# A routed expert layer: index table, gather and adding scatter in place of stored token rows

## The reference

```python
x = x + xattn(layernorm(x), ctx_768, ...)      # 16 heads over 257 context rows of 384
x = x + attn(layernorm(x), W_qkv, W_o)         # 16 heads of 32, within 32 tokens
x = x + ffn(layernorm(x), gate_w, gate_b, w1, b1, w2, b2, ln_g, ln_b)

def ffn(x, ...):                               # 8 experts, 2 per token
    logits = (x @ gate_w + gate_b) / 0.9
    topk_vals, topk_idx = top_k(logits, 2)
    gate_probs = softmax(where(chosen, logits, -inf))
    h = gelu(einsum('bsd,edf->bsef', x, w1) + b1)          # d 512, f 2048
    expert_out = einsum('bsef,efd->bsed', h, w2) + b2
    out = einsum('bse,bsed->bsd', gate_probs, expert_out)
    return (out - mean) / sqrt(var + 1e-5) * ln_g + ln_b
```

## Time and profile before

| | before |
|---|---|
| median of 3 runs | 1409.48 us (1407.01 to 1409.59) |
| profiled execution, own time | 1407.61 us |
| its span, first to last instruction | 1406.0 us |
| granted TensorE clock, mean | 0.980 |
| TensorE busy (PE) | 1312.6 us, 93% |
| VectorE / ScalarE / GpSimd busy | 1021.6 / 887.6 / 160.4 us |
| moved by DMA | 241.15 MB, 172 GB/s |

### The profile page before, as it was taken

One profiled execution on the slowest core, in us unless ns is written; L12 is line 12 of the kernel. 1 busy time (PEld: TensorE's weight loads), 2 busy tenths in 40 slices (PEclk: granted clock), 3 DMA queues, 4 the chain that ended last, 5 costly groups with the idle time before them and its releaser, 6 DMA issues.

```text
span 1406.0 us, 26769 instructions
## 1 busy us (share of the span) xinstructions
PE 1312.6 (93%) x8412; PEld 856.8 (61%) x8413; DVE 1021.6 (73%) x2163; ACT 887.6 (63%) x1427; POOL 160.4 (11%) x200
## 2 busy tenths in 40 slices
PE   5889999999999999999999789999999999999977
PEld 5658668687686686876866544555554545454532
DVE  5765777876868778768676558777777777778765
ACT  3567776676767776767677145666666666666630
POOL 1002002021020020211200200000000000000014
PEclk9998999999999999999999899999999999999997
DMA  9797245264272451732716980761617074300014
GB/s 366 284 357 259 86 164 203 64 251 145 94 254 82 172 194 64 265 131 96 252 61 226 367 311 17 298 251 62 265 48 278 35 288 176 140 22 22 15 46 149
DMA packets 70482, 241.15 MB, mean 172 GB/s; under 512 B 5422, under 2 KB 5532, under 8 KB 64292
## 3 DMA queue, kind: packets, MB, share of 16 engines
q1 hardware_dynamic: 57232, 156.77, 31.2%
q0 software_dynamic: 13184, 83.89, 15.6%
q10 hardware_dynamic: 28, 0.01, 0.0%
HBM read 177.73 MB, written 62.91 MB: 171 GB/s over the span
## 4 chain that ended last, share of the span: by engine, by line
PE 78%; DVE 8%; issue 5%; ACT 5%; DMA 2%; POOL 2%; ACTq 0%; DVEq 0%; SPq 0%
PE bank L1648 9%; PE bank L1606 8%; PE bank L743 6%; PE bank L745 6%; PE bank L744 6%; PE bank L723 6%; PE bank L724 6%; PE bank L725 5%; PE bank L1569 4%; PE bank L1674 4%; PE bank L1590 3%; PE bank L733 3%; PE bank L1615 2%; PE bank L1630 2%; PE bank L1696 2%
## 5 line engine op out<-in xcount | busy, mean ns | idle before, releaser
L1606 PE MATMUL bank<-moe_w 128*128 128x257 f32 x768 | 188.8, 383 | 6.4 <-DVE moe_w L1025 6.4
L1606 PEld LDWEIGHTS bank<-moe_w 128*128 128x128 f32 x768 | 137.5, 191 | 25.2 <-DVE moe_w L1025 5.8
L723 PE MATMUL bank<-moe_w,arena 128*128 x368 | 139.9, 380 | 0.0
L725 PE MATMUL bank<-moe_w,arena 128*128 x368 | 139.9, 380 | 0.0
L724 PE MATMUL bank<-moe_w,arena 128*128 x368 | 139.9, 380 | 0.0
L1648 PE MATMUL bank<-moe_w 128*128 128x512 f16 x384 | 114.5, 379 | 9.9 <-ACT moe_w L1082 7.0
L464 ACT ACTIVATE wosT<-moe_w,now_v_act 128x1024 f16 x92 | 100.7, 1141 | 27.5 <-PE bank L745 27.5
L554 DVE SCALAR_TENSOR_TENSOR arena<-bank,now_b,arena 128x512 f32<-128x512 f32 x92 | 69.0, 751 | 62.3 <-PE bank L725 55.7
L1068 ACT ACTIVATE moe_w<-bank,cols,ugain 128x512 f32<-128x512 f32 x96 | 74.6, 777 | 61.7 <-PE bank L1649 60.7
L1278 DVE TENSOR_TENSOR moe_w<-bank,moe_w 128x512 f16<-128x512 f32 (+1 forms) x96 | 65.4, 688 | 47.9 <-ACT moe_w L1082 45.6
L457 ACT ACTIVATE arena<-bank,now_h 128x512 f16<-128x512 f32 x92 | 63.6, 691 | 50.4 <-PE bank L733 34.8
(11 more groups left out here) (283 smaller groups left out, 3011.0 us busy)
## 6 DMA issues: line engine op xcount, KB each, us to landing
moe_w<-in_L_ffn_w_dram SPq DMA_DIRECT2D x46, 1024.0 KB, 6.3
moe_w<-w_halves POOLq DMA_DIRECT2D x8, 4096.0 KB, 13.0
moe_w<-in_L_ffn_w_dram POOLq DMA_DIRECT2D x8, 4096.0 KB, 24.5
w_halves<-moe_w SPq DMA_DIRECT2D x48, 512.0 KB, 4.7
xs_rows<-blocks SPq DMA_DIRECT2D x8, 2048.0 KB, 14.6
arena<-in_ctx_dram SPq DMA_DIRECT2D x32, 384.0 KB
arena<-in_L_ffn_w_dram SPq DMA_DIRECT2D x10, 1024.0 KB, 5.0
blocks<-in_L_ffn_w_dram SPq DMA_DIRECT2D x8, 1024.0 KB, 4.8
```

The source lines that it names most:

```text
L723: nc.tensor.matmul(bank[fb % 2][:, :], xT_low[:, k, :], high, start=(k == 0), stop=False)
L725: last = nc.tensor.matmul(bank[fb % 2][:, :], xT_high[:, k, :], low, start=False, stop=(k == KD - 1))
L1606: last = nc.tensor.matmul(bank[h][:, 0:KEYS], qkT[:, c, b, h * P:(h + 1) * P], cnT[:, b % 2, c, :], start=(c == 0), stop=(c == KC - 1))
```

## The change

- Groups: `y2` is stored once, in token order, to `xn_rows` (GpSimd). What is scattered by slot is an entry of 8 bytes: the token's index and its gate, into `slot_table`. The gates are computed per group (`gates`, `gate_exp`).
- Zeroing: instead of `xs_rows`, the accumulator `acc_rows` (1152 rows), the 128 spare rows of `xn_rows`, and the table is preset with indices of spare rows.
- Jobs: GpSimd loads 128 entries of the table per job (23 DMAs, the last 22 between the gathers of jobs 0 and 1), gathers the token rows by them, and adds the result rows into `acc_rows` by an indirect DMA with addition. VectorE adds the expert's bias in `y_copy` and multiplies by the gate in a further instruction (`y_gate`).
- Expert weights are loaded from SyncE's queue.
- End: SyncE loads the eight tiles of `acc_rows`; gathers, diagonal matrices and mixing matmuls are gone.

```diff
@@ moe_loads (SyncE) @@
+            sp.wait_ge(m_full, M_FILLS * GROUPS)
+            sp.wait_ge(sum2_done, KD * GROUPS)
+            for k in range(KD):
+                sp.wait_ge(halves_out[k], 32 * GROUPS)
+            expert_load(sp, 0)
             sp.wait_ge(b_full, B_FILLS * GROUPS)
+            b2_load(sp, 0)
...
+            sp.wait_ge(xs_in, 16)
+            sp.wait_ge(experts_in, 64)
+            expert_load(sp, 1)
+            b2_load(sp, 1)
+            for e in range(2, EXPERTS):
+                sp.wait_ge(experts_in, 64 * e)
+                ended = sp.value_load(end_i[0:1, e - 1:e], min_val=1, max_val=1 + FB * JOBS)
+                sp.wait_ge(mm2_done, ended)
+                expert_load(sp, e)
+                sp.wait_ge(mm2_done, ended + 1)
+                b2_load(sp, e)
+            sp.wait_ge(ys_stored, 16 * JOBS)
+            for t in range(GROUPS):
+                sp.dma_start(got[:, t, :], acc_dram[t * P:(t + 1) * P, :]).then_inc(gathered[t], 16)
@@ moe_pool (GpSimd) @@
+            def idx_load(j, done):
+                row = pool.value_load(job_rows[0:1, j:j + 1], min_val=0, max_val=ROWS // P - 1)
+                pool.dma_start(job_idx[:, j, :], table[bass.ds(row * P, P), :]).then_inc(done, 16)
+            def x_gather(j):
+                nc.gpsimd.indirect_dma_start(
+                    out=xs, out_offset=None, in_=xn_dram[:, :],
+                    in_offset=bass.IndirectOffsetOnAxis(ap=job_idx[:, j, 0:1].bitcast(U32), axis=0)).then_inc(xs_in, 16)
+            def y_add(j):
+                nc.gpsimd.indirect_dma_start(
+                    out=acc_dram[:, :], out_offset=bass.IndirectOffsetOnAxis(ap=job_idx[:, j, 0:1].bitcast(U32), axis=0),
+                    in_=ys, in_offset=None, compute_op=ALU.add).then_inc(ys_stored, 16)
             pool.wait_ge(jobs_ready, 1)
+            pool.wait_ge(scattered, 16 * GROUPS * TOPK)
+            pool.wait_ge(y2_stored, 16 * GROUPS)
+            idx_load(0, idx0_in)
+            pool.wait_ge(idx0_in, 16)
+            x_gather(0)
+            for j in range(1, JOBS):
+                idx_load(j, idx_in)
+            pool.wait_ge(idx_in, 16 * (JOBS - 1))
+            pool.wait_ge(xt_full, 1)
+            x_gather(1)
+            for j in range(JOBS):
+                if j + 2 < JOBS:
+                    pool.wait_ge(xt_full, j + 2)
+                    x_gather(j + 2)
+                if j > 0:
+                    pool.wait_ge(ys_stored, 16 * j)
+                pool.wait_ge(ys_out, j + 1)
+                y_add(j)
@@ SyncE, ahead of group 0 @@
-            for e in range(ZERO_FIRST):
-                zero_rows(e)
+            zero_rows(acc_dram[:, :], GROUPS + 1)
+            zero_rows(xn_dram[TOKENS:, :], 1)
+            sp.wait_ge(table_set, 1)
+            sp.dma_start(table.rearrange("(j p) k -> j (p k)", p=P), table_first).then_inc(xs_zeroed, 16)
@@ scatter (GpSimd) @@
+                pool.wait_ge(y_done, 2 * (g + 1))
+                nc.gpsimd.tensor_tensor(row_mark[:, :], half[:, 0:1], half[:, 0:1], ALU.add).then_inc(y2_seen, 1)
+                pool.dma_start(xn_dram[bass.ds(g * P, P), :], y2[:, :]).then_inc(y2_stored, 16)
                 pool.wait_ge(slots_ready, g + 1)
...
-                        out=xs_dram[:, :], out_offset=bass.IndirectOffsetOnAxis(ap=slot_now[:, k:k + 1], axis=0),
-                        in_=y2[:, :], in_offset=None).then_inc(scattered, 16)
+                        out=table[:, :], out_offset=bass.IndirectOffsetOnAxis(ap=slot_now[:, k:k + 1], axis=0),
+                        in_=entry[:, k, :], in_offset=None).then_inc(scattered, 16)
@@ gate_exp (ScalarE, between w_hi(g, 2) and w_hi(g, 3)) @@
+                act.wait_ge(gs_ready, g + 1)
+                nc.scalar.activation(ge[:, :], gs[:, :], ACT.Exp).then_inc(gexp_done, 1)
@@ gates (VectorE, ahead of place) @@
+                dve.wait_ge(gexp_done, g + 1)
+                link = chain(dve, rt_step, RT_LINKS * g + 5)
+                link(nc.vector.tensor_scalar(gsum[:, :], ge[:, :], 1.0, None, ALU.add))
+                link(nc.vector.reciprocal(entry_f[:, 0, 1:2], gsum[:, :]))
+                nc.vector.tensor_tensor(entry_f[:, 1, 1:2], ge[:, :], entry_f[:, 0, 1:2], ALU.mult)
+                nc.vector.tensor_copy(entry[:, :, 0], ids[:, bass.ds(g, 1)].to_broadcast([P, TOPK]))
@@ jobs (VectorE) @@
-                nc.vector.tensor_scalar(ys, Y[:, :], now_y[:, 0:1], None, ALU.mult).then_inc(ys_out, 1)
+                nc.vector.scalar_tensor_tensor(out=ys, in0=Y[:, :], scalar=now_y[:, 0:1], in1=b2_rows_at(slot),
+                                               op0=ALU.mult, op1=ALU.add).then_inc(ys_raw, 1)
+            def y_gate(j):
+                dve.wait_ge(ys_raw, j + 1)
+                dve.wait_ge(now_gate_ok, j + 1)
+                nc.vector.tensor_scalar(ys, ys, now_gate[:, 0:1], None, ALU.mult).then_inc(ys_out, 1)
...
                 y_scale_now(j, e)
+                if not first:
+                    y_gate(j - 1)
                 bias(j, 2, slot)
+                gate_now(j)
```

More of the change, by code:

```diff
@@ L670, in moe_dve @@
             h_lo(JOBS - 1, 3)
-            v_lo(JOBS - 1, 3, slot_of(JOBS - 1))
-            y_copy(JOBS - 1)
-            for t in range(GROUPS):
-                for k in range(TOPK):
-                    last = nc.vector.tensor_scalar(diags[t][k], ident[:, :], gp[:, t, k:k + 1], None, ALU.mult)
-            last.then_inc(diags_done, 1)
-            dve.wait_ge(pw_full, 1)
-            for i in range(2):
-                last = nc.vector.tensor_copy(pT8[:, 4 * i:4 * i + 4, :].rearrange("e t n -> e (t n)"), bank[2 + i][0:EXPERTS, :])
-            last.then_inc(pw_out, 1)
+            slot_before = slot_of(JOBS - 1)
+            v_lo(JOBS - 1, 3, slot_before)
+            y_copy(JOBS - 1, slot_before)
+            y_gate(JOBS - 1)
             dve.wait_ge(xb_done, 1)
@@ L692, in moe_dve @@
             for t in range(GROUPS):
-                mixed, m = bank[t], fin_mv[:, t % 2]
-                dve.wait_ge(mix_full, t + 1)
-                link(nc.vector.bn_stats(stats[:, :], mixed[:, :]))
+                mixed, m = got[:, t, :], fin_mv[:, t % 2]
+                dve.wait_ge(gathered[t], 16)
+                link(nc.vector.bn_stats(stats[:, :], mixed))
                 link(nc.vector.bn_aggr(m[:, 0:2], stats[:, :]))
@@ L699, in moe_dve @@
                     fin_out(t - 1)
-                nc.vector.scalar_tensor_tensor(out=fin[:, t, :], in0=mixed[:, :], scalar=m[:, 0:1], in1=lnrow[:, 0, :],
+                nc.vector.scalar_tensor_tensor(out=fin[:, t, :], in0=mixed, scalar=m[:, 0:1], in1=lnrow[:, 0, :],
                                                op0=ALU.subtract, op1=ALU.mult).then_inc(mix_used, 1)
@@ L777, in moe_pe @@
             mm2(JOBS - 1, 3)
-            pe.wait_ge(rows_in, 48)
-            pe.wait_ge(h_biased, FB * JOBS)
-            pe.wait_ge(hT_out, FB * JOBS)
-            pe.wait_ge(pw_ready, 1)
-            for t in range(GROUPS):
-                last = nc.tensor.transpose(bank[2 + t // 4][0:EXPERTS, (t % 4) * P:(t % 4 + 1) * P], pe_all[:, t, :], ident[:, :])
-            last.then_inc(pw_full, 1)
-            pe.wait_ge(pw_out, 1)
-            pe.wait_ge(diags_done, 1)
-            pe.wait_ge(ys_out, JOBS)
-            for t in range(GROUPS):
-                nc.tensor.matmul(bank[t][:, :], pT8[:, t, :], b2_sb[:, :], start=True, stop=False)
-            for t in range(GROUPS):
-                pe.wait_ge(gathered[t], 16 * TOPK)
-                nc.tensor.matmul(bank[t][:, :], diags[t][0], got[:, t, 0, :], start=False, stop=False)
-                nc.tensor.matmul(bank[t][:, :], diags[t][1], got[:, t, 1, :], start=False, stop=True).then_inc(mix_full, 1)
         def ctx_load(sp, g, b):
@@ L1175, in body @@
                     w_hi(g, 2)
+                if do_b:
+                    gate_exp(g - 1)
+                if do_a:
                     w_hi(g, 3)
@@ L1447, in body @@
                 if do_b:
+                    gates(g - 1)
                     place(g - 1)
```

201 lines of the change are left out of this document (67 added, 134 removed).

## The result

The kernel after takes 1414.10 us (median of six runs, 1412.35 to 1416.53) against 1409.53 before (six, 1407.01 to 1411.28): ratio 1.0032, interval 1.0021 to 1.0042. Timed again beside the last group of experiments it came to 1411.41 against 1409.70, ratio 1.0015 (1.0005 to 1.0025). So it is slower by 2 to 5 us. The forecast was 1406.6, faster by 2.9.

The account below looks back on a forecast made before the run. TensorE was taken to bound the job stretch, leaving group 0, first gather, first jobs and tail to matter. Terms -7.0 + 0 + 2.5 + 15.2 + 0 - 13.6 = -2.9 us gave 1406.6 us, range 1391 to 1417.

Parts of the forecast that it names:

- 1 zeroing: End of group 0: without the large zero stores the context load goes out earlier, ending waits; -7.0 us, bounds 5 and 7.6.
- 2 groups: Steady groups: VectorE's added gate work is covered by its idle time; cost 0, or 5 us if the cover fails.
- 3 first gather: Before job 0: scatter landing, register read, table load and gather in chain; +2.5 us, bounds -1 to +6.
- 4 table loads: Between gathers of jobs 0 and 1: 22 GpSimd read-and-load pairs of 1.4 us stall TensorE; +15.2 us with slower clock.
- 5 jobs: Jobs: VectorE's gate scaling and copy, and the adding scatter, fit into existing slack; cost 0.
- 6 tail: Kernel end: gathers and mixing matmuls go, an adding scatter of 6.2 us comes; -13.6 us, bounds -16 and -5.
- clock still falls: End of group 0: the zeroing gain's bound of 5 us, if TensorE's clock drops anyway.
- rival C: Jobs 0 to 1: table loads queue beside expert 1's load, 9.7 us each; stall 20, total +4.4, 1413.9 us; chance 0.20.

Follow-up runs that it names:

- after_again: The kernel after, unchanged, timed and profiled again: 1411.41 us, ratio 1.0015.
- sqrt_act: Kernel after with the last two of eight variance powers moved from GpSimd to VectorE's reciprocal and ScalarE's square root: 1407.74 us, ratio 0.9995.
- zero_spread: Kernel after with the zeroing of before put back in its old order, to a tensor nothing reads: 1416.05 us, ratio 1.0048.
- first_two_sp: Kernel after with 21 table loads behind the second gather, last two powers on ScalarE, jobs 0 and 1's table loads on SyncE: 1395.06 us, ratio 0.9898.
- rows_late: Kernel after with the broadcasts of expert 0's b2 and the two layer norm rows issued behind the first gather: 1411.46 us, ratio 1.0021.
- loads_behind: Kernel after with only job 1's table load ahead of the second gather, the other 21 behind it: 1402.36 us, ratio 0.9951.
- expert1_held: Kernel after with SyncE's load of expert 1 held until the second gather has landed: 1409.15 us, ratio 0.9999.

## Why the prediction was wrong

Prediction and profile (after against before) by its own terms:

```
term                          predicted   first profile   after_again
1 zeroing (start of proj 1)      -7.0          -3.6            -5.4
2 groups (proj 1 to mark 8)       0            +2.6            +6.9
3 first gather (mark 8 to job 0) +2.5          +5.4            +3.3
4 table loads (job 0 to job 1)  +15.2         +10.0           +10.0
5 jobs (to last matmul)           0            +0.5            +1.0
6 tail (to the end of VectorE)  -13.6         -14.6           -15.0
- end of VectorE to the end       0            +4.5            +4.5
sum                              -2.9          +4.8            +5.3
```

**The step that failed** is the last, which the sum did not have: it took "the final store and the end" of the earlier trace rows as fixed. The store did land 2.3 us behind VectorE as before, but GpSimd's drain had grown from 2.69 to 8.74 us and became what ends last. sqrt_act shows it: taking the last two powers off GpSimd brings the end back to the store. Without these 4.5 us the profile would give +0.3, no change. That it would come so near to -2.9 is in part luck: in the first profile terms 1 to 3 are 8.9 us above the forecast, term 4 is 5.2 below it, the tail 1.0 below. The two terms that were to carry the forecast, the pair of read and load and the adding scatter, both came out cheaper than taken; they are not what made it wrong.

**1.** The mechanism was right: the waits of 6.1 and 5.9 us went, and zero_spread brings them back. The size was too big. At equal early clock (after_again and zero_spread) the projections move by 5.7 us, the first mark by 5.1, the kernel by 4.7 (2.3 by the first ratio of after). Of the 2.5 us that the clock was to give back, only a part came: the 32 output projections still took 8.83 us against 9.90, although the gap ahead of them was down to 1.5. The bound of 5 "clock still falls" was the case. In the first profile the clock also fell at 34 and 57 us. It did so in three of the thirteen profiles of kernels with the change (granted clock 0.83 from 30 to 40 us, 1.00 in the other ten), and not when the same kernel ran again.

**2.** The cover for `gates` held: passes two to six keep 92.8 to 92.9 us. But the first pass of the loop takes 94.0 to 94.4 in place of 92.6, and 93.3 or more in every kernel with the change. There the stores of `w_halves` land 8.4 us after their issue (median; 5.0 before), and GpSimd starts clearing `blocks` at 231 in place of 227. The 16 DMA engines are fully busy meanwhile and move little: 99 GB/s from 220 to 230, where before they were busy for 0.57 of the time at 224 GB/s (223 to 230). The same is found behind the scatters of the later passes, more weakly each time, where it costs TensorE nothing: from 313 to 320 fully busy at 171 GB/s (before 0.60 at 243, 315 to 322), from 592 to 599 0.78 at 207 (before 0.59 at 236, 594 to 601). The 8-byte scatters land late in it themselves: after 14.3, 11.7 and 9.1 us for the first, second and fifth pair of them in after_again (the later of each pair), where the row scatters of before took 6.6, 7.3 and 7.1. So they are the suspect, but no run leaves them out, and the cause is not shown. A further 0.9 us goes between group 1's projections and the first mark, in both profiles of after; what takes it was not looked into. The rest of this term is the last leg, and only in after_again. It took 35.2 us in the one profile of before, 35.0 in the first of after and 33.4 to 39.7 in all kernels with the change, longest where the clock was lowest; whether the change costs 1 or 2 us there these runs cannot say.

**3.** The chain was right, its scatter too short: I took 3.8 us for its landing, where first_two_sp shows 6.3, without GpSimd in the wait, and taking the broadcasts out of its way gained nothing that shows (rows_late). What it lands behind was not settled. The term's upper bound of 6 held.

**4.** Right in kind, and it was the largest loss, as loads_behind shows. The pair took 1.155 us where I had 1.4: the register read with its address is 0.6 us on GpSimd, not the 0.8 taken from VectorE. That is 5.4 us less over 22 loads. Against that the last load landed after 5.3 us rather than 2.7, beside expert 1's load: 12.7 - 5.4 + 2.6 = 9.9, and the trace has 10.0. Of the 2.5 us for the halved clock behind the stall, 0.5 to 1.0 at most is seen in the jobs' row of the table: the clock was 0.85 from 852 to 862, but loads_behind, without the stall and at 1.00 there, needs 524.3 us from job 1 to the last matmul, after 523.2. So rival C's mechanism was there at a third of the 9.7 us a load that it had for its price (expert1_held: 3.2 us; median landing 5.5 against 2.0). What the prediction worked out from packets, that C would then not occur, did not come out for these loads. The floor of about 600 ns that the Trainium skill puts on a tensor load ("DMA: Bandwidth & Descriptors", Latency and other measured facts) would have given this price: the trace agrees with it on GpSimd.

**5 and 6.** As predicted. The jobs keep their length (523.2 us from job 1 to the last matmul, before 522.7), and the tail up to VectorE is 1 us better than forecast: the adding scatter takes 1.55 us of issue and 4.80 us in all to land, not 6.2.

## What to carry to other kernels

Small transfers cost their engine's time one after the other: put ahead of a gather only the rows that this gather needs, and the rest where the engine idles. That one move, with the last two powers taken off the engine that closed last, and the first two loads on another queue (a step within the noise, 0.9917 to 0.9898), turns a change that lost 0.15 to 0.3% into one that gains 1.0% (1395.06 us, ratio 0.9898). When an edit moves many transfers to an engine, look at that engine's drain on the closing line, and compare the end of the span with the last landing before trusting a tail.

## What the runs showed of the hardware that I had not expected

GpSimd's drain is long, and the same in each kernel to 0.01 us: 8.73 with all table loads on it, 8.57 with two fewer, 6.85 with 23 fewer. That is 0.08 us for each load issued before, some of them more than 500 us earlier. With each load its register read and its code went too, so the runs do not say which of them counts; the two powers less in sqrt_act changed nothing. The load count alone does not bridge the way to the 2.69 us of before; what the other transfers add stays open.

An adding scatter of 128 rows of 2 KB takes 1.59 us to issue and 4.8 to land, a plain one 0.99 and 2.8. A scatter of 8 bytes a row landed no sooner than one of 2 KB a row: 6.3 us after its issue in first_two_sp against 4.87 in the earlier trace rows, and in the steady groups up to 14.3 us (after_again) against 7.3.
